# Middle stage of a fused two-layer block: one long product per slot, the query products moved to the small products' bank, turned heads kept for eight heads

## The reference

```python
# x: (16, 112, 256), ctx: (16, 375, 256)
x = x + tanh(g_xattn[0]) * L0_xattn(layernorm(x), ctx)      # first stage: 16 heads of 16
x = x + tanh(g_ffn[0])   * L0_ffn(layernorm(x))             # first stage: 8 experts
# middle stage: 16 heads of 64
xn, ln_lat = layer_norm(ctx, g1, b1), layer_norm(layernorm(x), g2, b2)
q = ln_lat @ Wq                                             # 112 x 1024
k, v = split(concat([xn, ln_lat]) @ Wkv)                    # 487 x 1024 each
w = softmax(where(mask, q @ k.T / 8, -max))                 # per head 112 x 487
x = x + tanh(g_xattn[1]) * ((w @ v) @ Wout)
# then: logits of 8 experts, top 2 of them, and each token's row sent to its experts (last stage)
x = x + tanh(g_ffn[1])   * L1_ffn(layernorm(x))             # last stage: 8 experts of 512
```

## Time and profile before

| | us |
|---|---|
| median of 3 runs | 1486.99 (1485.8 to 1488.27) |
| profiled execution | 1494.09 |
| its span | 1492.5 |
| first stage | about 0 to 464 |
| middle stage, setup and first batch's items | about 464 to 516.5 |
| middle stage, batches 0 to 15 | about 516.5 to 1253 |
| routing of the last batch, last stage | about 1253 to 1492.5 |

### The profile page before, as it was taken

One profiled execution on the slowest core, in us unless ns is written; L12 is line 12 of the kernel. 1 busy time (PEld: TensorE's weight loads), 2 busy tenths in 40 slices (PEclk: granted clock), 3 DMA queues, 4 the chain that ended last, 5 costly groups with the idle time before them and its releaser, 6 DMA issues. The chain is left out here.

```text
span 1492.5 us, 43700 instructions
## 1 busy us (share of the span) xinstructions
PE 1278.8 (86%) x13508; PEld 918.0 (62%) x13508; DVE 1126.8 (75%) x3238; ACT 953.7 (64%) x2456; POOL 822.4 (55%) x1172
## 2 busy tenths in 40 slices
PE   5999999999973989897897979989799976288995
PEld 3788888888751346554564546545555555188994
DVE  4899999999973488786886868868778773378772
ACT  3888888878871377675775657666667663155663
POOL 3644454444453465675775666656757764145664
PEclk8999999999995999998998989989999996589997
DMA  5333333333301276776766776757767685663323
GB/s 167 102 114 96 123 95 117 114 103 117 95 11 38 75 124 141 139 145 114 130 147 123 137 138 118 152 118 140 136 121 149 127 174 96 223 217 53 59 38 75
DMA packets 303993, 175.39 MB, mean 118 GB/s; under 512 B 250234, under 2 KB 291586, under 8 KB 300720
## 3 DMA queue, kind: packets, MB, share of 16 engines
q1 hardware_dynamic: 287632, 130.94, 40.9%
q0 software_dynamic: 13168, 35.80, 9.4%
q10 hardware_dynamic: 3024, 6.47, 1.5%
HBM read 64.48 MB, written 41.96 MB: 71 GB/s over the span
## 5 line engine op out<-in xcount | busy, mean ns | idle before, releaser
L1451 PE MATMUL b_ps_p<-b_tok_s,w_s 128*128 128x112 f16 (+1 forms) x1536 | 238.6, 308 | 46.5 <-DVE b_v_s L1733 42.8
L1277 POOL TENSOR_TENSOR b_halves<-b_prob,b_halves 112x487 f16<-112x487 f32 x128 | 147.9, 1156 | 140.5 <-ACT b_halves L1636 140.3
L1630 ACT ACTIVATE b_prob<-b_prob,b_top 112x487 f32<-112x487 f32 x256 | 178.1, 696 | 50.9 <-DVE b_top L1738 48.5
L1451 PEld LDWEIGHTS b_ps_p<-b_tok_s,w_s 128*128 128x128 f16 x1536 | 112.0, 101 | 156.6 <-issue 82.6
L1738 DVE CUSTOM_DVE_ANT_0 b_prob<-b_ps_s,b_keep 112x487 f32<-112x487 f32 x256 | 167.4, 655 | 40.7 <-POOL b_keep L1260 23.4
L1451 PE MATMUL b_ps_p<-w_s,b_tok_s 128*128 128x512 f16 (+1 forms) x768 | 187.7, 380 | 0.0
L1636 ACT ACTIVATE b_halves<-b_prob 112x487 f16<-112x487 f32 x256 | 155.3, 607 | 32.6 <-DMA b_pT<-b_halves 32.0
L701 ACT ACTIVATE a_prob<-a_prob,a_top 112x375 f32<-112x375 f32 x256 | 156.4, 611 | 4.5 <-DVE a_top L837 3.4
L837 DVE CUSTOM_DVE_ANT_0 a_prob<-a_ps_s,a_keep 112x375 f32<-112x375 f32 x256 | 138.5, 541 | 24.3 <-PE a_ps_s L593 21.7
L1552 PEld LDWEIGHTS b_ps_o<-b_v_s,b_pT 128*128 128x128 f16 (+1 forms) x3072 | 124.5, 100 | 40.8 <-DMA b_pT<-b_halves 18.1
L1552 PE MATMUL b_ps_o<-b_v_s,b_pT 128*128 128x64 f16 (+1 forms) x3072 | 135.2, 195 | 13.2 <-DMA b_pT<-b_halves 13.1
(11 more groups left out here) (258 smaller groups left out, 3001.0 us busy)
## 6 DMA issues: line engine op xcount, KB each, us to landing
xs<-a_blank SPq DMA_DIRECT2D x14, 1032.0 KB, 4.0
c_w_pool<-w_split SPq DMA_DIRECT2D x8, 1600.0 KB, 11.0
b_wch_f<-in_w_experts POOLq DMA_DIRECT2D x32, 384.0 KB, 4.5
w_split<-b_wch_s POOLq DMA_DIRECT2D x32, 384.0 KB, 4.3
a_ctx_f<-in_ctxT SPq DMA_DIRECT2D x16, 375.0 KB, 3.6
a_k_stack<-a_k_s SPq DMA_DIRECT2D x64, 93.8 KB, 2.8
b_ctx_t<-in_ctx SPq DMA_DIRECT2D x16, 375.0 KB
c_xt<-xs SPq DMA_DIRECT2D x35, 129.0 KB, 2.7
```

Source lines behind the costliest of these rows:

```text
L1277: pool.tensor_tensor(halves[:, h % RING, LO, 0:NK], prob[:, h % RING, 0:NK], halves[:, h % RING, HI, 0:NK], ALU.subtract).then_inc(s_lo[1], 1)
L1451: last = pe.matmul(out, sta(a, k), mov(m, k), start=(k == 0 and n == 0), stop=(k == tiles - 1 and n == 2))
L1630: act.activation(prob[:, h % RING, 0:NK], prob[:, h % RING, 0:NK], ACT.Exp, bias=top[:, h % RING:h % RING + 1], scale=-1.0, accum_out=sums ...
```

## The change

It does six things, all in the middle stage.

1. The items get a written order `ITEMS`: k0 to k3, q0, k4, q1, k5, k6, k7, v0 to v7. The two query items go to ps_x, in slots 3 and 4 of `XSLOT`; the 16 others alternate over the two banks ps_p, one in each slot.
2. An item waits for the item that last used its own bank (`before_bank`), over batch ends too. For k = 0 that is v6, no longer v7.
3. The lent bank's waits count the queries (`lent_before` and `lend`).
4. `halves` and `pT` are rings of `TURN` = 8 heads; `prob` stays at 4. `high_half` waits for the turn of the head eight before, and `turn` waits in addition until the turn four before has landed.
5. POOL: chunk 0 is split in slot 2 and stored in slot 4, chunk 1 split in 8 and stored in 12; `deviation` moves from slot 5 to 4, `aim_rows` from 6 to 5, `send_rows` from 8 to 6.
6. The setup's small buffers b2_f and b2_s lie in the row buffers `xr`.

```diff
-        halves = sb("halves", [T, RING, 2, NB1 * KB1], F16)
-        pT = sb("pT", [128, RING, 2, NB1, 128], F16)
+        TURN = 8
+        halves = sb("halves", [T, TURN, 2, NB1 * KB1], F16)
+        pT = sb("pT", [128, TURN, 2, NB1, 128], F16)
...
+        ITEMS = [("k", 0), ("k", 1), ("k", 2), ("k", 3), ("q", 0), ("k", 4), ("q", 1), ("k", 5), ("k", 6), ("k", 7)]
+        ITEMS += [("v", n) for n in range(2 * NB1)]
+        def before_bank(k):
+            n = [i for i in range(k) if ITEMS[i][0] != "q"]
+            return n[-2] + 1 if len(n) > 1 else len(n) - 1
...
-        for s, n in enumerate([2, 2] + [1] * 14):
-            PSLOT[s] = list(range(k, k + n))
-            k += n
+        for s in range(H):
+            PSLOT[s] = [k]
+            k += 2 if ITEMS[k + 1:k + 2] and ITEMS[k + 1][0] == "q" else 1
...
-        XSLOT = {1: ("h", 0), 2: ("r", 0), 6: ("h", 1), 8: ("n", 0), ...
+        XSLOT = {1: ("h", 0), 2: ("r", 0), 3: ("q", 0), 4: ("q", 1), 6: ("h", 1), 8: ("n", 0), ...
...
-                need_all(sp, settled, (s_lo[h % 2], H // 2, b, h // 2 + 1), (s_pv, H, b, h - RING + 1))
+                need_all(sp, settled, (s_lo[h % 2], H // 2, b, h // 2 + 1), (s_pv, H, b, h - TURN + 1),
+                         (s_turned[h % RING], 16 * (H // RING), b, 16 * (h // RING)))
...
-                        if s == 6:
-                            aim_rows(b - 2)
-                        if s == 8:
-                            send_rows(b - 2)
-                    if s in (0, 4):
-                        split_chunk(b, par, s // 4)
-                    if s in (2, 5):
-                        store_chunk(b, par, s // 4, pair)
+                        if s == 5:
+                            aim_rows(b - 2)
+                        if s == 6:
+                            send_rows(b - 2)
+                    if s == 2:
+                        split_chunk(b, par, 0)
+                    if s == 4:
+                        store_chunk(b, par, 0, pair)
...
+                    if s == 8:
+                        split_chunk(b, par, 1)
...
+                    if s == 12:
+                        store_chunk(b, par, 1, pair)
...
-                ps = ps_p[k % 2]
-
-                need(pe, s_ifree, PI, c, max(k - 1, 0))
+                ps = product_bank(k)
+                kind, n = ITEMS[k]
+
+                if kind != "q":
+                    need(pe, s_ifree, PI, c, before_bank(k))
...
+                if nq and ahead(b, 1):
+                    need(pe, s_ifree, PI, b + 1, nq)
+                if kind == "q":
+                    item(b + 1, 1 - par, ITEMS.index((kind, k)))
...
-                need(act, s_turned[h % RING], 16 * (H // RING), b, 16 * (h // RING))
-                act.activation(halves[:, h % RING, HI, 0:NK], prob[:, h % RING, 0:NK], ACT.Copy).then_inc(s_hi, 1)
+                need(act, s_turned[h % RING], 16 * (H // RING), b, 16 * ((h - TURN) // RING + 1))
+                act.activation(halves[:, h % TURN, HI, 0:NK], prob[:, h % RING, 0:NK], ACT.Copy).then_inc(s_hi, 1)
```

## The result

| | us | ratio to the kernel before (95%) |
|---|---|---|
| before | 1487.6 (1485.8 to 1488.3, 4 runs) | |
| after | 1473.6 (1470.9 to 1477.8, 4 runs) | 0.991 (0.9881 to 0.9939) |

What follows compares the result with a forecast made beforehand. TensorE was taken as the busiest engine, VectorE close behind, with TensorE's waits at batch starts and loop boundaries to win. 10.8 + 5 + 19.5 + 4 - 1 - 2.5, say 36 us, gave 1451 us from 1487; range 1438 to 1463.

Steps and rivals of the forecast that it cites:

- the 0.85 that I named as a sign: Middle stage: forecast wrong if VectorE's busy share goes over 0.85 with TensorE waiting for b_top.
- Part 1: Batch starts: k0 waits for v6, not v7, slot 0 has one item; 10.8 + 5 (clock) + 19.5 us won.
- the setup's 1: Queries through ps_x: in the setup q0 must follow n2's reading, 1 us more.
- The five loop boundaries: Loop boundaries: four long ones win 4.3 us each, the fifth 2.3, together 19.5 us (8 to 34).
- The nine ordinary ones: Ordinary batch starts: about 1.2 us each, 10.8 us, plus 5 us of clock at four of them.
- TensorE gets all of it back: Rival: clock returns sooner at five loop boundaries, ordinary boundaries give their full 2.3 us; 1429 us, chance 0.17.
- Part 2: Queries through ps_x: same work, costing the wait counted at the batch starts and 1 us more in the setup.
- It would be wrong if these reach 1.5 us a batch: Sign: q's waits in ps_x and the ranks' longer wait for b_oT, each expected under 0.7 us.
- Part 3: Rings of eight: in batch 15 ACT's waits for turns vanish, TensorE's remain in part; 4 us won (0 to 8).
- Part 4: POOL's moved slots: a low half beside a split costs 0.5 us at five loop boundaries, 2.5 us lost.
- The 7 us that I had worked out from that rule: POOL's slots: by the lock-out rule low halves lose 9.7 us instead of 2.5, the sum 7 us smaller; set aside.
- VectorE binds: Rival: VectorE full from slot 2 to 9 in every batch, waits come back; 12 us won, 1475 us, chance 0.13.

Runs made afterwards that it cites:

- d: Kernel before with the items' part alone (one long product per slot, wait per bank, queries in the lent bank), rings of four, POOL's old slots: 1439.6 us.
- a: The changed kernel with all of POOL's slots as they were before: 1435.4 us, ratio 0.966 to before.
- k: Against a: only the rows' steps (aim_rows, send_rows) moved to the new slots 5 and 6, splits and stores in the old slots: 1456.7 us.
- o: Against a: middle stage's loop written out, and each of a chunk split's two instructions issued as four over quarters of the columns: 1414.5 us.
- g: The changed kernel with VectorE's normalise issued in slot 6 instead of 7, POOL's new slots kept: 1494.7 us.
- n: The changed kernel with each of a chunk split's two instructions issued as four over quarters of the columns, in the same slot: 1449.5 us.

## Why the prediction was right in sign and wrong in size

**What bounds the kernel.** That no wait can be taken off TensorE without asking after VectorE was right, and I then asked it only for the batch's start. VectorE became the one that is waited for, at 607 of 719.5 us. That is a share of 0.84, just under the 0.85 that I named as a sign; the share alone would not have told.

**Part 1, ordinary and loop boundaries, with the clock (35.3 of the forecast, 34.3 less the setup's 1).** The mechanism was right and its size too small: d gives 48. TensorE's idle time is 34.7 us less and its busy time 12.3. Where they come from can be read batch by batch, from the fifth scores of one batch to the fifth of the next. The windows over the boundaries of batches 8 (loop) and 9 (ordinary), in before and then in d:

```profile
859.04:910.46 51.42, 43.51 (x438) 26.19 (x436) 37.01 (x98) 30.96 (x72) 31.24 (x50) 0.90 0.65 124
910.46:954.70 44.24, 40.88 (x437) 25.45 (x435) 36.85 (x96) 30.62 (x71) 31.39 (x48) 1.00 0.75 143
```

```profile
833.54:881.50 47.96, 42.23 (x437) 26.29 (x434) 36.61 (x96) 30.82 (x71) 32.16 (x50) 0.96 0.72 140
881.50:922.86 41.36, 40.40 (x437) 25.60 (x435) 36.55 (x96) 30.70 (x72) 31.21 (x48) 1.00 0.77 146
```

The five loop boundaries give 19.0 us together, where the forecast had 19.5. The nine ordinary ones give 28.8, 2.6 to 5.1 each, where the forecast had 15.8 with the clock: this is the term that was too small. At batch 9 the 2.9 us are 2.4 of idle and 0.5 of busy time. In before, TensorE stood 2.1 us there for v7, 0.7 for VectorE's reading of the turned tokens and 0.5 for turned heads; in d the one wait left in this stretch is that of the ranks, 0.9. The forecast counted only the first of the three as won, and put on 0.3 us for the second query, which is not in this stretch (the queries' waits are 5.0 us over the stage in d). TensorE's busy time is 6.1 us less at the four ordinary boundaries that had the low clock, forecast 5, and 1.2 less at each loop boundary. It is also 0.5 less at each of the other ordinary ones, with the clock at 1.00 in both kernels, which no run explains. The condition of the rival "TensorE gets all of it back" (1429), k1 in 1.3 us at the loop boundaries, did not come: in d k1 takes 2.19 to 2.62 us at all five. Its full ordinary boundaries did (25.6 with the clock, measured 28.8), and with POOL's slots out of the way a came to 1435, so it was the nearer of the two on this part, for half of its reason.

**Part 2, queries in the lent bank.** The waits for q stay at 2.4 us in all. The ranks' wait, forecast at 0.65 a batch, is 1.65 in batch 7 after, behind the low half of 1.84 us, so the excess belongs to part 4. Over the stage it is 15.9 us after and 11.3 in a, of which 2.9 stood in before as well. "It would be wrong if these reach 1.5 us a batch" named the right row, but the mean, with the queries' 2.4 us 1.3 a batch, stays under it.

**Part 3, rings of eight.** Forecast 4, measured 3.7 and 4.2. ACT's waits vanished and TensorE's remained in part, as written.

**Part 4, POOL: the step that failed.** "A low half on VectorE beside a split takes 1.01 us instead of 0.66; I count 0.5 us for five loop boundaries, 2.5 us lost" measured 38 us. Two things were wrong in it. I took 0.35 us from the one row at hand, in which the two met only at their edge, for the price of meeting. POOL's timeline of the kernel before, which I had not set beside the earlier trace rows, shows the edge:

```profile
852.60 1.65 POOL L1316 TENSOR_TENSOR b_wch_s<-b_wch_f,b_wch_s 128x768 f16<-128x768 f32 x1 [0.15 <-POOL b_wch_s L1314]
```

The subtraction ran until 854.25, the low half from 853.76 to 854.77: it began near the end of POOL's instruction and ended 0.52 us after it, as the long ones in k and o do. And I looked only at the slots that the splits came into at a loop boundary, not at what else they would meet: chunk 1's new slot lies beside the normalise in every batch, and the rows' steps, "more than ten slots until somebody needs them", push two low halves of POOL against one of VectorE's. The Trainium skill, page "SBUF — State Buffer", section "SBUF: two separate sides", which I had weighed and set aside, says that of a VectorE instruction with two SBUF inputs or in a two-port mode and a GpSimd instruction, whichever starts first gets the shared pair of ports for the whole instruction and the other blocks. The runs agree as to the whole instruction: the normalises end 0.15 us after POOL's third instruction, quarters give 24 us back, and no VectorE instruction that reads PSUM grew beside POOL (0.65 to 0.69 us for each of 242 subtractions of k and v). As to who starts first, the rows do not bear it out at this distance: in k VectorE's low half started 0.04 us before POOL's and was the one that waited. Whether the normalise runs in a two-port mode, no trace here shows; that it waits, g and n do. The 7 us that I had worked out from that rule were still too small by far, since I had applied it to five low halves only. And the opening, by which the engines meet only at semaphores, is wrong for these two: no semaphore stands between the normalise and the split.

**The sum by what was measured.** 48 for the items, 4 for the ring, less 38 for POOL is 14 us. The three are the steps of one chain of kernels (before, d, a, after), so that they add up is no proof of its own. VectorE binds (1475) was the rival that named the time, by luck and for a reason other than its own: VectorE was not full, its instructions grew.

## What to carry to other kernels

Before moving long POOL instructions, list for each what VectorE runs in SBUF alone beside it, at the new place as at the old, and price a meeting at the whole rest of POOL's instruction, and of the next one where it follows closely. If they must meet, POOL's in pieces can help (24 us in n), but need not (the low halves in o). A busy sum of VectorE that rises with the same count of instructions is the first sign. Where a wait and a branch lie together, write the loop out once to see which of them holds.

## What the runs showed of the hardware

- VectorE and POOL hold each other up in SBUF by whole instructions, and not strictly in turn: two of POOL's went ahead of one of VectorE's in g and k, and in o the running quarter and three more. It holds for VectorE's normalise (0.40 us alone, up to 2.70 in g) and for the low half, which reads two SBUF tiles (0.66 alone, 2.76 in k), and for the other engine too: in a, POOL's part of a split took 1.30 us instead of 0.82 where VectorE's low half had started 0.04 us before it.
- Instructions of VectorE that read PSUM ran beside any of POOL's at their usual length (256 maxima of the scores at 0.63 to 0.67 us in the kernel after).
- At the branch back of a loop VectorE stood for 5.7 to 6.3 us here, and TensorE for 2.0 to 2.6 us, in before and after once for 5.0 and 5.2; straight code over 16 batches showed no such gap.
